# A row-by-row convolution sweep on TensorE: mixed column tiles, a two-row loop and two state slots

## The chip, the core and the metric

One core of a Trainium2 chip runs the kernel. The metric is the device time of one execution in microseconds (us); lower is better. Three executions of the kernel before are given by their median.

## The reference

The model has two layers, on an input of 8 images x 32 channels x 64 x 64 pixels. Layer 0 is a spectral convolution and a mixture of experts over tokens; layer 1 is a convolution in four directional sweeps and the same kind of experts. The change touches the four sweeps alone:

```python
def _sweep(x, w, b, axis, reverse):
    rows = jnp.moveaxis(x, axis, 0)
    if reverse:
        rows = rows[::-1]
    def step(prev, row):
        new = row + jax.nn.relu(_conv1d(prev, w, b))   # 32 channels to 32, 9 taps along the row
        return (new, new)
    _, rest = jax.lax.scan(step, rows[0], rows[1:])
    ...
out = _sweep(x, w_d, b_d, axis=2, reverse=False)
out = _sweep(out, w_u, b_u, axis=2, reverse=True)
out = _sweep(out, w_r, b_r, axis=3, reverse=False)
out = _sweep(out, w_l, b_l, axis=3, reverse=True)
```

A row depends on the row before it, so the 63 steps of a sweep, and the four sweeps, run one after the other.

## The kernel before, in words

Before the sweeps the kernel does layer 0 and the layer norm of layer 1; after them the second mixture of experts. Both parts stay as they are. Each engine has its own program, and semaphores tie them together.

**A row's state.** A row has 64 pixels of 32 channels for 8 images. Four neighbouring pixels (`Q` = 4) lie on the partitions with their channels (4 x 32 = 128), the 16 groups of four (`HO`) lie along the free dimension, with a column of zeros at either side. The state of a row is one of four slots of the tile `state` in SBUF (names print it as RE, of which it is a part), each of 8 images x 18 columns; `state_slot(s, u)` picks the slot by the row's number modulo four.

**A step on TensorE (PE).** The 8 images are two chains of four (`CHAINS`). For a chain, the nine taps become three matmuls of a 128 x 128 banded weight (`conv_sb[:, s, d]`, d = 0, 1, 2) with the previous state shifted by d columns, 4 images x 16 columns = 64 streamed columns. They add up in a PSUM bank (`conv_bank`, two banks a chain, in turns). Each matmul is issued as two column tiles of `OC` = 64 output rows (L717). The data are fp32. The step of a chain waits for the chain's state of the row before (`s_st`) and for the bias in its bank (`s_seed`, L713), and its last matmul raises `s_cv`. PE's program of the sweeps is written out: 4 x 63 rows x 2 chains.

**The other engines.** VectorE (DVE) does one `scalar_tensor_tensor` a chain and row (L1114): relu of the bank plus the row of the source image, into the next state slot; it raises `s_st`. ScalarE (ACT) then writes the bias into the bank that this frees (L851, `seed`). GpSimd (POOL) copies each finished row from its slot to the destination image (L391, `archive`, `s_arc`); in the last sweep ScalarE does it (L865, `s_arl`). Before VectorE writes over a slot, it waits for the archive of the row that was in it, four rows back.

**Between sweeps.** Sweeps 1 and 2 run along the height, 3 and 4 along the width. DMAs issued on SP's queue (L317, `move_rows`, and POOL for some of the last batch) turn the image meanwhile in four batches of 5, 5, 4 and 2 groups of four rows (`MOVED`), 16 DMAs each; each batch waits for the rows of sweep 2 that it needs. Sweep 3 starts with a wait for them (`wait_columns`). Behind sweep 4 the result is turned back the same way (L328).

Other lines in the rows below: L454 keeps PE active with bf16 matmuls of 128 columns (`keep_warm`); L508 is the mixing of the spectrum, in column tiles of 64; L636 pools tokens, in column tiles of 64 with 32 streamed columns; L652 spreads one row over 32 output rows; L663 and L669 are the experts' small products, in tiles of 64 and 32 output rows; L492, L532, L583 and L646 are full-width transforms and transposes.

Of the kernel before, what the change touches and what calls it, by code (L numbers as in the profile page):

```python
# [8 lines left out]
B, C, H, W = 8, 32, 64, 64  # L9
P = 128  # L10
# [4 lines left out]
Q = 4  # L15
HO = H // Q
# [4 lines left out]
WRUN = W // NW  # L21
MO = P // 2
CHAINS = ((0, 4), (4, 8))
OC = P // 2
SEEDS = ((0, 1), (1, 2))
KYC = 4
NCH = KY // KYC
# [1 line left out]
WCOLS = 2 * X8 * KYC * 2 * C  # L29
# [11 lines left out]
def build_kernel(nc, x_in, dft, wspec, conv_w, conv_b, gate_w, gate_b, w1, w2, b2, own, out):  # L41
# [5 lines left out]
    with ExitStack() as ctx:  # L47
        def sb(name, shape, dt=F32):
            return ctx.enter_context(nc.sbuf_tensor(name, shape, dt))

        def sem(name):
            return ctx.enter_context(nc.semaphore(name))
# [4 lines left out]
        RE = sb("RE", [P, 3 * WCOLS])  # L57
# [6 lines left out]
        conv_sb = sb("conv_sb", [P, 4, 3, P])  # L64
# [51 lines left out]
        s_st, s_cv = sem("state_ready"), sem("conv_ready")  # L116
        s_seed, s_arc, s_pad = sem("bias_in_bank"), sem("row_archived"), sem("state_zeroed")
        s_bits, s_arl = sem("banks_written"), sem("last_rows_archived")
# [8 lines left out]
        def blk(region, n):  # L127

            return region[:, n * P:(n + 1) * P]

        def banks(b0, nb):
            return PS[:, b0:b0 + nb, :].rearrange("p k c -> p (k c)")
# [21 lines left out]
        X3 = RA[:, :].rearrange("p (k t i w o) -> p k t i w o", k=NW, t=BH, i=Q, w=WRUN)  # L154


        state = RE[:, 2 * WCOLS + 3072:2 * WCOLS + 3072 + 4 * B * (HO + 2)].rearrange(
            "p (s b v) -> p s b v", s=4, b=B)

        def by_run(ap, k):  # L160

# [96 lines left out]
        def row_count(s, t):  # L258

            return 127 * (s // 2) + 63 * (s % 2) + t + 1  # L260

        def state_count(s, t, c):

            return len(CHAINS) * (row_count(s, t) - 1) + c + 1

        def seed_of(c):

            return next(i for i, (c0, c1) in enumerate(SEEDS) if c0 <= c < c1)

        def state_slot(s, u):  # L270

            return (u + 3 * (s % 2)) % 4

        def conv_bank(s, u, c):

            b0, b1 = CHAINS[c]
            c0, c1 = SEEDS[seed_of(c)]
            bank = 2 * c0 + (s + u + 1) % 2 * (c1 - c0) + c - c0
            return PS[:, bank, 0:(b1 - b0) * HO].rearrange("p (b v) -> p b v", v=HO)

        def archive_row(eng, s, q, u):

            eng.wait_ge(s_st, state_count(s, Q * q + u, len(CHAINS) - 1))
            return row_at(DST[s], s, q, u), state[:, state_slot(s, u), :, 1:1 + HO]

        def row_at(image, s, q, u):

            if s % 2:
                q, u = HO - 1 - q, Q - 1 - u
            if image is XF:  # L290
                return XF[:, Q * q + u]
            if image is XW:
                return XW[:, u, :, q, :]
            return XV[:, u, :, :, q]
# [8 lines left out]
        def wait_columns(eng, j):  # L303

            share = sum(on_pool(j, i) for i in range(Q))
            eng.wait_ge(s_ph[j], 16 * (Q * len(MOVED) - share))
            eng.wait_ge(s_php[j], 16 * share)
# [101 lines left out]
        def _(pe):  # L409
# [60 lines left out]
            for l in range(2):  # L470
                m = pe.matmul(PS[:, 6 + l, 0:BL * NE], centre, gate_sb[:, l, :], start=True, stop=True)
# [50 lines left out]
            for c in range(NCH):  # L522
# [5 lines left out]
                for w, full, read in ((1, s_t1, s_tmp), (0, s_t0, s_comb)):  # L528
                    if c >= 2:
                        pe.wait_ge(read, c - 1)  # L530
                    for x in range(X8):
                        m = pe.transpose(blk(banks(4 * (c % 2) + 2 * w, 2), x), Z[:, c, x, w], ident)  # L532
# [172 lines left out]
            for bank in range(2 * len(CHAINS)):  # L705
                m = pe.matmul(PS[:, bank, 0:P], warm[:, :], warm[:, :], start=True, stop=True)
            m.then_inc(s_bits, 1)
            for s in range(4):
                def step(q, u):
                    for c, (b0, b1) in enumerate(CHAINS):  # L710
                        pe.wait_ge(s_st, state_count(s, Q * q + u - 1, c))
                        if c == SEEDS[seed_of(c)][0]:
                            pe.wait_ge(s_seed, len(SEEDS) * (63 * s + Q * q + u - 1) + seed_of(c) + 1)  # L713
                        for d in range(3):
                            prev = state[:, state_slot(s, u - 1), b0:b1, d:d + HO]
                            for o in range(0, P, OC):
                                m = pe.matmul(conv_bank(s, u, c)[o:o + OC], conv_sb[:, s, d, o:o + OC], prev,  # L717
                                              start=False, stop=(d == 2), skip_group_check=True)
                        m.then_inc(s_cv, 1)

                for r in range(1, H):
                    step(r // Q, r % Q)

            experts(1)

# [148 lines left out]
        def _(dve):  # L874
# [103 lines left out]
            for g in range(8):  # L978
                dve.wait_ge(s_df, g + 1)
                for o, i in if2_pairs(g):  # L980
                    m = dve.tensor_copy(o, i)
# [112 lines left out]
            for s in range(4):  # L1094
                if s % 2 == 0:
                    if s == 0:
                        dve.wait_ge(s_pad, 1)
                        dve.wait_ge(s_fd, 16)
                    else:
                        wait_columns(dve, 0)  # L1100
                    for b0, b1 in CHAINS:
                        dve.tensor_copy(state[:, 0, b0:b1, 1:1 + HO], row_at(SRC[s], s, 0, 0)[:, b0:b1, :]).then_inc(s_st, 1)  # L1102
                else:
                    dve.wait_ge(s_arc, 63 * (s - 1) + 62)

                def step(q, u):
                    for c, (b0, b1) in enumerate(CHAINS):
                        r = Q * q + u
                        dve.wait_ge(s_cv, len(CHAINS) * (63 * s + r - 1) + c + 1)
                        if c == 0 and s == 3 and r > Q:  # L1110
                            dve.wait_ge(s_arl, r - Q)
                        elif c == 0 and 63 * s + r > Q:
                            dve.wait_ge(s_arc, 63 * s + r - Q)
                        dve.scalar_tensor_tensor(out=state[:, state_slot(s, u), b0:b1, 1:1 + HO], in0=conv_bank(s, u, c),  # L1114
                                                 scalar=0.0, in1=row_at(SRC[s], s, q, u)[:, b0:b1, :],
                                                 op0=ALU.max, op1=ALU.add).then_inc(s_st, 1)

                for r in range(1, H):
                    if s == 2 and r < Q:
                        wait_columns(dve, r)  # L1120
                    step(r // Q, r % Q)
# [71 lines left out]
```

## Time and profile before

| | us |
|---|---|
| Median of three executions | 623.08 (619.97 to 624.44) |
| Profiled execution, whole | 622.25 |
| Profiled execution, span from first to last instruction | 620.4 |
| PE busy | 565.0 |
| VectorE busy | 365.3 |
| ScalarE busy | 318.9 |
| GpSimd busy | 95.2 |
| Mean granted clock of TensorE, share of 2.4 GHz | 0.961 |

Times in the profile are us from the span's start, unless marked ns. "PE" is a matmul's record, "PEld" that of a weight load. A record of a matmul lasts from its start to its modelled end, so records of matmuls that follow one another overlap, and the sum of a group is counted without the overlap. Where instructions of one line are merged in an order of time, the row gives the first start and the time to the last end, and xN counts the records.

### The profile page before, as it was taken

The numbers are of one execution on the slowest core, as the hardware profiler recorded it, in microseconds if no ns is written. First come the engines' busy times: TensorE is split into PE (matmuls) and PEld (weight loads), VectorE is DVE, ScalarE is ACT, GpSimd is POOL, SyncE is SP. The second block draws the span as 40 slices with busy tenths as digits, with TensorE's granted clock in tenths as the row PEclk, the third lists the DMA queues.
The fourth block names the chain that finished last, engine by engine and source line by source line (L and its number), as shares of the span: only waits on it lengthen the run. The fifth ranks groups of instructions, "written<-read, shape, count | busy, mean of one in ns | idle before, by whom it ended". The sixth has DMA issues, their size and how long they took to land.

```text
span 620.4 us, 22679 instructions
## 1 busy us (share of the span) xinstructions
PE 565.0 (91%) x9860; PEld 505.4 (81%) x9860; DVE 365.3 (59%) x825; ACT 318.9 (51%) x842; POOL 95.2 (15%) x218
## 2 busy tenths in 40 slices
PE   8978887999997999996999999939999999985997
PEld 8978787999996986896888888838888888974873
DVE  3647989656549825555455445515555545598626
ACT  4766988542368401254444444414445777659510
POOL 4000000000021000000333333333332033320000
PEclk9999999999998889998999999969999999987979
DMA  9830772060000000000000013340000144500007
GB/s 357 318 136 1 274 287 125 1 271 1 1 2 2 1 21 1 0 1 0 5 4 4 4 39 75 83 85 4 5 3 5 33 78 75 97 1 1 2 3 270
DMA packets 52650, 41.53 MB, mean 67 GB/s; under 512 B 47558, under 2 KB 47686, under 8 KB 51334
## 3 DMA queue, kind: packets, MB, share of 16 engines
q1 hardware_dynamic: 52024, 39.10, 19.6%
q8 instruction: 79, 1.29, 0.9%
q0 software_dynamic: 384, 0.59, 0.5%
q10 hardware_dynamic: 144, 0.39, 0.2%
q14 instruction: 19, 0.16, 0.1%
HBM read 27.49 MB, written 4.19 MB: 51 GB/s over the span
## 4 chain that ended last, share of the span: by engine, by line
PE 73%; DVE 16%; ACT 5%; SPq 3%; issue 2%; POOL 1%; DMA 0%; ACTq 0%
PE PS L717 35%; PE PS L433 6%; PE PS L686 5%; DVE RB L958 4%; PE PS L454 4%; SPq L317 3%; PE PS L508 3%; DVE sums L997 3%; PE PS L636 3%; PE PS L583 2%; PE PS L532 2%; DVE RCD L1009 2%; PE PS L539 2%; PE PS L553 2%; PE PS L613 2%
## 5 line engine op out<-in xcount | busy, mean ns | idle before, releaser
L717 PE MATMUL PS<-RE,conv_sb 128*64 128x64 f32 x6048 | 229.3, 226 | 11.2 <-DVE RE L1102 9.2
L717 PEld LDWEIGHTS PS<-RE,conv_sb 128*64 128x64 f32 x6048 | 198.8, 138 | 41.7 <-DVE RE L1102 9.8
L851 ACT COPY PS<-convb_sb 128x64 f32<-128x64 f32 x504 | 108.1, 215 | 117.9 <-DVE RE L1114 77.9
L1114 DVE SCALAR_TENSOR_TENSOR RE<-PS,RCD 128x64 f32<-128x64 f32 x252 | 56.7, 225 | 57.0 <-PE PS L717 40.5
L391 POOL COPY RCD<-RE 128x128 f32<-128x128 f32 x126 | 37.3, 296 | 176.8 <-DVE RE L1114 176.8
L1114 DVE SCALAR_TENSOR_TENSOR RE<-PS,RE 128x64 f32<-128x64 f32 x126 | 32.3, 258 | 29.2 <-PE PS L717 19.4
L780 ACT COPY RB<-PS 32x256 f32<-32x256 f32 x64 | 41.9, 655 | 6.9 <-PE PS L492 6.1
L1114 DVE SCALAR_TENSOR_TENSOR RE<-PS,RB 128x64 f32<-128x64 f32 x126 | 28.4, 225 | 28.1 <-PE PS L717 19.9
L958 DVE COPY RB<-PS 32x256 f32<-32x256 f32 x64 | 41.7, 652 | 5.1 <-PE PS L492 4.3
L454 PE MATMUL PS<-warm 128*128 128x128 bf16 x468 | 38.1, 254 | 7.1 <-ACT RCD L820 4.4
L454 PEld LDWEIGHTS PS<-warm 128*128 128x128 bf16 x468 | 35.0, 116 | 8.1 <-ACT RCD L820 4.7
L508 PE MATMUL PS<-RE,RB 128*64 128x64 f32 x1024 | 32.2, 223 | 8.7 <-DVE RCD L967 3.7
L884 DVE TENSOR_REDUCE sums<-RE 128x32 f32<-128x1024 f32 x16 | 19.4, 1218 | 33.8 <-ACT RE L752 33.8
L508 PEld LDWEIGHTS PS<-RE,RB 128*64 128x64 f32 x1024 | 31.0, 138 | 10.0 <-issue 5.4
L752 ACT ACTIVATE RE<-PS 128x1024 f32<-128x1024 f32 x16 | 16.2, 1021 | 33.6 <-PE PS L433 33.5
L384 POOL TENSOR_TENSOR RE<-RA 128x1024 f32<-128x1024 f32 x3 | 5.7, 1892 | 177.4 <-ACT RA L813 177.4
L433 PEld LDWEIGHTS PS<-dft_sb,RCD 128*128 128x128 f32 x128 | 30.5, 328 | 0.9 <-issue 0.5
L433 PE MATMUL PS<-dft_sb,RCD 128*128 128x128 f32 x128 | 30.8, 396 | 0.0
L741 ACT COPY RCD<-PS 128x256 f32<-128x256 f32 (+1 forms) x40 | 24.7, 692 | 11.1 <-PE PS L697 6.0
L686 PE MATMUL PS<-RCD,espread 128*128 128x512 f32 x64 | 30.4, 631 | 0.0
L799 ACT COPY RB<-PS 128x512 f32<-128x512 f32 (+1 forms) x24 | 16.2, 736 | 26.1 <-PE PS L539 26.1
L613 PE MATMUL PS<-proj,RA 128*128 128x192 f32 x128 | 23.5, 346 | 3.0 <-DVE RA L334 2.6
(118 smaller groups left out, 773.9 us busy)
## 6 DMA issues: line engine op xcount, KB each, us to landing
RE<-wspec SPq DMA_DIRECT2D x8, 2048.0 KB, 8.3
RA<-x_in SPq DMA_DIRECT2D x8, 512.0 KB, 7.6
RCD<-x_in SPq DMA_DIRECT2D x1, 4096.0 KB, 13.4
out<-RA SPq DMA_DIRECT2D x8, 512.0 KB, 2.7
RCD<-RB SPq DMA_DIRECT2D x58, 64.0 KB, 2.6
RE<-RCD SPq DMA_DIRECT2D x32, 80.0 KB, 2.6
RE<-RCD SPq DMA_DIRECT2D x16, 64.0 KB, 2.1
conv_sb<-conv_w SPq DMA_DIRECT2D x1, 768.0 KB, 20.0
```

The lines of the kernel that those rows point to most:

```text
L391: pool.tensor_copy(o, i).then_inc(s_arc, 1)
L433: m = pe.matmul(blk(ln_slot(g), n), src, centre, start=True, stop=True)
L454: pe.matmul(PS[:, bank, 0:P], warm[:, :], warm[:, :], start=True, stop=True)
L508: m = pe.matmul(o[:, x % 2, y], XB[:, c % 2, x, 2 * y + a].rearrange("p r q b -> p (r q b)"), WR[:, c % 3, a, x, y, :], start=True, stop=True)
L613: m = pe.matmul(PS[:, 4 * (g % 2) + n // 2, 192 * (n % 2):192 * (n % 2) + 192], src, proj[:, l, :], start=True, stop=True)
L686: pe.matmul(PS[:, 4 + k % 4, :], espread[:, BL * bh:BL * bh + BL, :].rearrange("p b o -> p (b o)"), rhs, start=True, stop=True).then_inc(s ...
L717: m = pe.matmul(conv_bank(s, u, c)[o:o + OC], conv_sb[:, s, d, o:o + OC], prev, start=False, stop=(d == 2), skip_group_check=True)
L741: m = act.copy(o, i)
L780: m = act.copy(o, i)
L851: act.copy(banks_of, convb_sb[:, s:s + 1].unsqueeze(2).to_broadcast([P, c1 - c0, n])).then_inc(s_seed, 1)
L958: m = dve.tensor_copy(o, i)
L1114: dve.scalar_tensor_tensor(out=state[:, state_slot(s, u), b0:b1, 1:1 + HO], in0=conv_bank(s, u, c), scalar=0.0, in1=row_at(SRC[s], s, q, u ...
```

## The change

`OC`, the output rows of a column tile, becomes a tuple: the matmul of d = 0 is issued as four tiles of 32, those of d = 1 and 2 stay two tiles of 64. PE's program of a sweep becomes row 1, written out, and a hardware loop of 31 passes over two rows each, in which the numbers waited for are worked out from the loop's register. As the slot's address must be fixed within the loop's body, the state has two slots instead of four, and VectorE waits for the archive of two rows back. The whole diff:

```diff
--- before.py
+++ after.py
@@ -21,7 +21,7 @@
 WRUN = W // NW
 MO = P // 2
 CHAINS = ((0, 4), (4, 8))
-OC = P // 2
+OC = (P // 4, P // 2, P // 2)
 SEEDS = ((0, 1), (1, 2))
 KYC = 4
 NCH = KY // KYC
@@ -154,8 +154,8 @@
         X3 = RA[:, :].rearrange("p (k t i w o) -> p k t i w o", k=NW, t=BH, i=Q, w=WRUN)
 
 
-        state = RE[:, 2 * WCOLS + 3072:2 * WCOLS + 3072 + 4 * B * (HO + 2)].rearrange(
-            "p (s b v) -> p s b v", s=4, b=B)
+        state = RE[:, 2 * WCOLS + 3072:2 * WCOLS + 3072 + 2 * B * (HO + 2)].rearrange(
+            "p (s b v) -> p s b v", s=2, b=B)
 
         def by_run(ap, k):
 
@@ -269,7 +269,7 @@
 
         def state_slot(s, u):
 
-            return (u + 3 * (s % 2)) % 4
+            return (u + s) % 2
 
         def conv_bank(s, u, c):
 
@@ -706,20 +706,22 @@
                 m = pe.matmul(PS[:, bank, 0:P], warm[:, :], warm[:, :], start=True, stop=True)
             m.then_inc(s_bits, 1)
             for s in range(4):
-                def step(q, u):
+                def step(r, odd=1):
                     for c, (b0, b1) in enumerate(CHAINS):
-                        pe.wait_ge(s_st, state_count(s, Q * q + u - 1, c))
+                        pe.wait_ge(s_st, state_count(s, r - 1, c))
                         if c == SEEDS[seed_of(c)][0]:
-                            pe.wait_ge(s_seed, len(SEEDS) * (63 * s + Q * q + u - 1) + seed_of(c) + 1)
+                            pe.wait_ge(s_seed, len(SEEDS) * (63 * s + r - 1) + seed_of(c) + 1)
                         for d in range(3):
-                            prev = state[:, state_slot(s, u - 1), b0:b1, d:d + HO]
-                            for o in range(0, P, OC):
-                                m = pe.matmul(conv_bank(s, u, c)[o:o + OC], conv_sb[:, s, d, o:o + OC], prev,
+                            prev = state[:, (s + odd - 1) % 2, b0:b1, d:d + HO]
+                            for o in range(0, P, OC[d]):
+                                m = pe.matmul(conv_bank(s, odd, c)[o:o + OC[d]], conv_sb[:, s, d, o:o + OC[d]], prev,
                                               start=False, stop=(d == 2), skip_group_check=True)
                         m.then_inc(s_cv, 1)
 
-                for r in range(1, H):
-                    step(r // Q, r % Q)
+                step(1)
+                with pe.Fori(1, H // 2) as pair:
+                    step(2 * pair, 0)
+                    step(2 * pair + 1, 1)
 
             experts(1)
 
@@ -1107,10 +1109,10 @@
                     for c, (b0, b1) in enumerate(CHAINS):
                         r = Q * q + u
                         dve.wait_ge(s_cv, len(CHAINS) * (63 * s + r - 1) + c + 1)
-                        if c == 0 and s == 3 and r > Q:
-                            dve.wait_ge(s_arl, r - Q)
-                        elif c == 0 and 63 * s + r > Q:
-                            dve.wait_ge(s_arc, 63 * s + r - Q)
+                        if c == 0 and s == 3 and r > 2:
+                            dve.wait_ge(s_arl, r - 2)
+                        elif c == 0 and 63 * s + r > 2:
+                            dve.wait_ge(s_arc, 63 * s + r - 2)
                         dve.scalar_tensor_tensor(out=state[:, state_slot(s, u), b0:b1, 1:1 + HO], in0=conv_bank(s, u, c),
                                                  scalar=0.0, in1=row_at(SRC[s], s, q, u)[:, b0:b1, :],
                                                  op0=ALU.max, op1=ALU.add).then_inc(s_st, 1)
```

## Rows read from the trace of the kernel before

**Rows 1.** The page: busy time by engine, and the chain that ended last by line.

```profile
PE 565.0 (91%) x9860; PEld 505.4 (81%) x9860; DVE 365.3 (59%) x825; ACT 318.9 (51%) x842; POOL 95.2 (15%) x218
...
PE PS L717 35%; PE PS L433 6%; PE PS L686 5%; DVE RB L958 4%; PE PS L454 4%; SPq L317 3%; PE PS L508 3%; DVE sums L997 3%; PE PS L636 3%; PE PS L583 2%; PE PS L532 2%; DVE RCD L1009 2%; PE PS L539 2%; PE PS L553 2%; PE PS L613 2%
```

**Rows 2.** Stretches (length, busy PE, PEld, DVE, ACT, POOL, PEclk, DMA, GB/s).

```profile
291.70:403.90 112.20, 112.08 (x3002) 97.73 (x3004) 56.05 (x250) 53.85 (x252) 36.69 (x124) 1.00 0.12 30
403.90:413.80 9.90, 0.83 (x24) 0.69 (x24) 0.83 (x5) 0.75 (x4) 4.37 (x9) 0.77 0.45 102
413.80:531.90 118.10, 116.36 (x3024) 100.35 (x3024) 60.80 (x253) 67.47 (x310) 30.44 (x68) 0.98 0.19 32
```

**Rows 3.** The page's costliest groups: busy, mean ns | idle before, releaser.

```profile
L717 PE MATMUL PS<-RE,conv_sb 128*64 128x64 f32 x6048 | 229.3, 226 | 11.2 <-DVE RE L1102 9.2
...
L851 ACT COPY PS<-convb_sb 128x64 f32<-128x64 f32 x504 | 108.1, 215 | 117.9 <-DVE RE L1114 77.9
L1114 DVE SCALAR_TENSOR_TENSOR RE<-PS,RCD 128x64 f32<-128x64 f32 x252 | 56.7, 225 | 57.0 <-PE PS L717 40.5
...
L1114 DVE SCALAR_TENSOR_TENSOR RE<-PS,RE 128x64 f32<-128x64 f32 x126 | 32.3, 258 | 29.2 <-PE PS L717 19.4
```

**Rows 4.** Instructions in order of time, four narrow windows from 310.48 to 311.22.

```profile
310.31 0.23 DVE L1114 SCALAR_TENSOR_TENSOR RE<-PS,RCD 128x64 f32<-128x64 f32 x1 [0.32 <-PE PS L717]
...
310.39 0.47 PE L717 MATMUL PS<-RE,conv_sb 128*64 128x64 f32 x3
...
310.59 0.14 PEld L717 LDWEIGHTS PS<-RE,conv_sb 128*64 128x64 f32 x2
...
310.66 0.23 DVE L1114 SCALAR_TENSOR_TENSOR RE<-PS,RCD 128x64 f32<-128x64 f32 x1
310.70 0.46 PE L717 MATMUL PS<-RE,conv_sb 128*64 128x64 f32 x10
...
310.95 0.30 POOL L391 COPY RCD<-RE 128x128 f32<-128x128 f32 x1 [0.60 <-DVE RE L1114]
...
311.21 0.23 DVE L1114 SCALAR_TENSOR_TENSOR RE<-PS,RCD 128x64 f32<-128x64 f32 x1 [0.32 <-PE PS L717]
```

**Rows 5.** In order of time, PE: one group of L508, one of L583.

```profile
87.39 3.95 PE L508 MATMUL PS<-RE,RB 128*64 128x64 f32 x128
...
152.62 1.95 PE L583 MATMUL PS<-dft_sb,RB 128*128 128x128 f32 x16
```

**Rows 6.** In order of time: changes of tile width; clock at the last.

```profile
110.05 0.43 PE L508 MATMUL PS<-RE,RB 128*64 128x64 f32 x8
...
110.41 0.14 PEld L532 LDWEIGHTS PS<-dft_sb,RCD 128*128 128x128 f32 x1
...
598.87 0.36 PE L669 MATMUL PS<-hid,w_sb 128*32 128x8 f32 x4
...
599.16 0.10 PEld L454 LDWEIGHTS PS<-warm 128*128 128x128 bf16 x1
...
588.87 0.40 PE L652 MATMUL PS<-rs_row,ones 1*32 1x128 f32 x2
...
589.20 0.20 PEld L636 LDWEIGHTS PS<-RE,RB 128*64 128x64 f32 x4 [0.20 <-issue]
...
588.60:589.30 0.70, 0.70 (x10) 0.34 (x7) 0.32 (x1) 0.00 (x0) 0.00 (x0) 1.00 0.00 0
```

**Rows 7.** Line L713: durations in ns (min/median/max), first and last start.

```profile
L713 PEldq EVENT_SEMAPHORE  x504: 51/51/51, 291.7 to 531.0; - x168
```

**Rows 8.** SP's issues from 398.15 on; waits (us, times, longest) at 403:421.

```profile
398.22 19.76 SPq L317 DMA_DIRECT2D RE<-RCD  x26
...
DVE RE L1102 <- DMA RE<-RCD: 8.6, 1, 8.6
...
DVE RE L1114 <- DMA RE<-RCD: 4.0, 3, 1.9
```

**Rows 9.** Busy time and granted clock, 597.1 to 599.1 us (columns as rows 2).

```profile
597.10:599.10 2.00, 2.00 (x36) 1.80 (x33) 0.00 (x0) 0.00 (x0) 0.00 (x0) 0.50 0.04 8
```

## The prediction

> **What bounds the kernel now.** I read the page first, then the sweeps' windows, then single instructions of one row. TensorE is busy for 91% of the span, and the sweep's matmuls, L717, alone are 35% of the chain that ended last [rows 1]. The four sweeps last from 291.7 to 403.9 us and from 413.8 to 531.9 us, and the stretch in between is a wait for DMAs [rows 2, 8]. In the sweeps PE shows as busy all the time [rows 2], with 6048 matmul records of 221 ns [rows 3], and the reader must not stop there: the records overlap, so a full PE row says nothing of how fast instructions start.
>
> Single instructions say it. In a row at 310.4 us, chain 1's last matmul starts at 310.39 and takes 221 ns; VectorE's instruction on it starts at 310.66 and ends at 310.89; the row's archive copy starts at 310.95. Chain 0's VectorE instruction ends at 310.54 (310.31 + 0.23) and its next weight load starts at 310.59, while PE had started no matmul since 310.39 [rows 4]. So PE has a hole of some 0.20 us in each row, and each chain of images runs in its own closed loop: release to first weight load 0.05; weights to first matmul 0.05 (load at 310.59, the second pass at 310.70, less 0.058); six passes 0.058 apart with two tiles side by side, 5 x 0.058 + 0.007 = 0.30; drain of the last matmul 0.22; hand-over to VectorE 0.05; VectorE 0.225. Sum 0.895 us, and VectorE's starts agree (310.31, then 311.21). The 0.058 is from L508, which has the same tile shape: 64 pairs of tiles start within 3.95 - 0.22 = 3.73 us [rows 5]. PE itself is taken for 2 x 0.35 = 0.70 us of the 0.895. The third sweep's VectorE instruction takes 258 instead of 225 ns [rows 3], so a row there is 0.929 us.
>
> **Column tiles, first matmul of a step.** Instructions: an fp32 matmul leaves two load/matmul pairs (6048 records for 252 x 2 x 3 x 2 calls). A chain's step goes from 12 to 16 pairs. Gain: the exposed weight load halves. L652 loads 32 columns; it starts at 588.87 and its second and last pass starts at 589.27 - 0.27 = 589.00, 0.13 later [rows 6]. A pass of 128 columns is some 0.11 apart from the next (L583: (1.95 - 0.27) / 15 [rows 5]), and the clock was full [rows 6], so that load took 0.02 to 0.03 against 0.05 for 64 columns: 0.02 us a row. Later loads hide behind passes in either shape. The fourth tile starts 3 x 0.007 after the first where the second started 0.007 after it, which takes 0.014 back. Net gain between 0.01 and 0.023 us a row.
>
> Cost: the array changes its tile width inside each step (32 to 64 columns) and again between the chains' steps (64 to 32). At each change of width in this trace, PE stands still [rows 6]. 64 to 128: the last L508 matmul starts at 110.05 + 0.43 - 0.22 = 110.26, the next load at 110.41, 0.15 later. 32 to 128: L669 (a 0.20 record) at 598.87 + 0.36 - 0.20 = 599.03, L454's load at 599.16, 0.13, and L454 there waits for no semaphore. 32 to 64: L652 at 589.00, load at 589.20, 0.20, of which its 128 streamed columns are 0.05 more than 64; the trace names "issue" as what it waited for. Within one width the next load starts within 0.01 of the matmul. L652 also has one row, so no row shows 32 against 64 columns at 128 rows, which is what the change makes. Bounds for one switch: nothing, and 0.20 us. I take 0.15, by the nearest rows with 32 or 64 streamed columns.
>
> The Trainium skill, page "TensorEngine Tiling (Array Packing)", section "Key Properties", says that changing the tiling mode, and not merely the tile, drains TensorE. The rows above agree as far as they go. By that rule both switches are paid and the time is the forecast below; without it, it is rival (a).
>
> A chain's step on PE then is: load 0.03; four tiles, two passes, 0.058 + 3 x 0.007 = 0.08; switch 0.15; load 0.05; four passes 3 x 0.058 + 0.007 = 0.18; together 0.49 us to its last matmul, and 0.15 to the next chain's load: 0.64. (If eight pairs in four tiles go no faster than two tiles' mean of 0.029 a pair, the 0.08 becomes 0.20 and a row 0.25 longer; I take 0.08, since tiles start 0.007 apart [rows 4].) Two chains: 1.27 us a row. The closed loop would be 0.49 + 0.22 + 0.05 + 0.225 + 0.05 = 1.04. So the limit moves from the loop to PE, and a row takes 1.27.
>
> Sum: three sweeps of 63 rows at 1.272 - 0.896 = 0.376, 71.1 us; the third at 1.272 - 0.929 = 0.343, 21.6 us; together 92.7.
>
> Taken back around it. Sweep 2's last two batches of row moves are issued on SP without a gap from 398.2 to 418 us, 0.65 us each [rows 8]. The third batch is released 8 rows before the end of the sweep; with rows 0.376 longer the sweep ends 3.0 us later against that queue, and the 8.6 us wait for columns shrinks by as much. The 4.0 us of DMA waits in the next three rows swallow another 1.0. The last column moves behind sweep 4, issued on the same queue, give perhaps 1 us in the same way (an estimate from the 3.0). Net 92.7 - 5 = 88.
>
> **Two state slots.** VectorE now waits for the archive of row r - 2. Row r - 2 was archived 0.36 us after its state was done (310.89, 310.95 + 0.30 = 311.25), and the chain 0 instruction after the next (311.21 + 0.895) starts near 312.1, so the wait is met 0.85 us early [rows 4]; ScalarE's copies in sweep 4 stand behind its seeds of 0.215 [rows 3]; with a copy as long as GpSimd's 0.30 it is still some 0.7 us early. Longer rows add to it. Cost nothing; a missing cover would queue the chain 1 instruction, its seeds and its archive behind it.
>
> **The loop of two rows.** No row has a wait against a register or a taken branch. PE has 504 semaphore instructions in the sweeps at 51 ns [rows 7], today not in the closed loop, since a load starts 0.05 after VectorE's end. Now each chain's two waits need sums on the sequencer. Bounds: zero, if the sequencer runs ahead; three such 51 ns instructions per step in the loop, 0.15 us. In the forecast PE is the limit, and the next chain's state is ready at 0.22 + 0.05 + 0.225 + 0.05 = 0.545 after its own last matmul, 0.09 before PE's 0.64 are over. So 0.09 of the 0.15 is covered and 0.06 a step, 0.12 a row (30 us), is the worst; I take zero and keep the rest for the range. Queued behind such a wait is all of that chain's step and, PE being in order, the other chain's.
>
> Forecast: 622.25 + 88 = 710 us on the profiled execution's own time, which lies 0.8 below the median of 623.08.
>
> **Rivals.** (a) No drain between 32 and 64 columns, and register waits hidden: both are widths of a divided array, and the only 32 to 64 row in the trace also changes its rows. Then 0.01 to 0.023 us a row are gained, 252 rows give 2.5 to 5.8 us: about 618, not slower. It decides if one switch costs under about 0.02 us. (b) No drain, but the waits enter the closed loop: 252 x (0.15 - 0.01) = 35, less 2 at the SP queue: 655. (c) Only the switch inside the step drains: loop 1.04 beats PE's 2 x 0.49, so 189 x 0.14 + 63 x 0.14 (VectorE's 258 ns count again) = 36, less 2: 656. (d) With PE standing still more, its clock falls to the lower level, 1.2 GHz: the granted clock was 0.50 from 597.1 to 599.1 us, after L663's and L669's short matmuls [rows 9]. For it speaks that, in the sum above, PE streams for less of a row; against it, the clock is 1.00 in the sweeps even now with holes [rows 2]. Passes and loads would double, 0.34 a step: some 0.68 x 252 = 170 more, 880.
>
> The Trainium skill, page "TensorE: Matmul & The Clock Gate", section "Wait — 56ns, not 53.3ns?", says that matmuls never start less than about 25 ns apart. The sweep's rows have tiles 7 ns apart, so the trace does not bear it out for separate tiles; by the rule the four tiles' two passes would take 0.18 and the row 0.19 more.
>
> **How the numbers follow.** Forecast's mechanism 60%, with a range of its own of 690 to 750 (each of a row's four switches 0.02 shorter: 20 us less; waits exposed: 30 more, and 0.01 on each switch). Rivals (b) and (c) together 18%; (a) 20%; (d) 2%. To leave out no more than two in ten the range runs from 640 to 755. A measurement of this kernel tells about 1% from no change. Faster by over 1% would need 6.2 us, above (a)'s upper bound, 0.04; within 1%, 0.16; slower, 0.80.
>
> **What would show it.** Right: at the sweep's matmuls a load of 64 columns that starts 0.15 us after the last 32-column matmul, and one of 32 columns 0.15 after the last of 64; VectorE's starts 1.27 apart per chain; 8064 records; less of the wait at 404 us. Wrong: rows at 0.88 with no hole between widths (a), holes ahead of the first load only, longer than 0.05 after VectorE's end (b), a hole only inside the step (c), PEclk near 5 in the sweeps (d).

## The result and the profile after

The changed kernel takes 891.54 us (median of four executions, 889.3 to 894.49) against 622.79 us (619.97 to 624.44, four) for the kernel before: a ratio of 1.4322, with a 95% interval of 1.4282 to 1.4362. The forecast was 710, its range ended at 755. What happened is rival (d), to which the prediction gave 2% and 880 us. The profiled execution took 892.41 us.

The page of the changed kernel: its busy time, the granted clock in 40 slices, the chain by line, and the groups of the sweep's matmul, its weight load and VectorE's instruction.

```profile
PE 842.4 (95%) x11876; PEld 668.1 (75%) x11876; DVE 364.8 (41%) x825; ACT 319.4 (36%) x842; POOL 94.1 (11%) x218
...
PEclk9999999998999555555555555555555555558798
...
L717 PE MATMUL PS<-RE,conv_sb 128*32 128x64 f32 (+1 forms) x8064 | 503.5, 321 | 4.8 <-DVE RE L1104 4.1
L717 PEld LDWEIGHTS PS<-RE,conv_sb 128*32 128x32 f32 (+1 forms) x8064 | 358.7, 179 | 149.6 <-issue 85.9
...
L1116 DVE SCALAR_TENSOR_TENSOR RE<-PS,RCD 128x64 f32<-128x64 f32 x252 | 56.5, 224 | 195.7 <-PE PS L717 195.7
```

Busy PE rose from 565.0 [rows 1] to 842.4 us, and VectorE's instruction, 224 ns against 225 [rows 3], now has 195.7 instead of 57.0 us of idle time ahead of it. The clock row tells the rest at a glance: 5 in every slice from the start of the sweeps to their end. The mean length of a matmul's record goes with it, from 226 [rows 3] to 321 ns. The stretches of the changed kernel (columns as in rows 2) show the same number by number.

```profile
288.00:291.00 3.00, 1.37 (x30) 0.98 (x32) 0.52 (x3) 1.82 (x8) 0.00 (x0) 1.00 0.00 0
291.00:292.50 1.50, 1.50 (x32) 1.10 (x32) 0.26 (x2) 0.43 (x2) 0.29 (x1) 0.55 0.00 0
...
291.70:541.00 249.30, 249.30 (x3994) 177.71 (x3991) 55.78 (x249) 53.75 (x250) 36.62 (x125) 0.50 0.06 15
541.00:549.00 8.00, 3.64 (x64) 2.52 (x62) 1.24 (x5) 0.64 (x3) 4.60 (x9) 0.50 0.35 61
549.00:801.00 252.00, 251.67 (x3993) 180.03 (x3990) 62.83 (x252) 67.45 (x309) 31.65 (x70) 0.50 0.08 14
```

The sweeps begin near 290 us. The clock is 1.00 up to 291 us, 0.55 in the next 1.5 us, and 0.50, TensorE's lower level of 1.2 GHz, for the 509 us from 291.7 to 801. All four executions have a mean clock of 0.69 to 0.694, so it fell in each. The stretch of 249.3 us holds 249 VectorE instructions, two a row: 2.00 us a row, where it was 0.896.

Single instructions of one chain's step, from three narrow windows of the changed kernel's timeline:

```profile
350.10 0.57 PE L717 MATMUL PS<-RE,conv_sb 128*64 128x64 f32 x3
350.35 0.13 PEld L717 LDWEIGHTS PS<-RE,conv_sb 128*32 128x32 f32 x1
...
350.35 0.44 PE L717 MATMUL PS<-RE,conv_sb 128*32 128x64 f32 x8
...
350.72 0.19 PEld L717 LDWEIGHTS PS<-RE,conv_sb 128*64 128x64 f32 x2 [0.17 <-issue]
...
351.10 0.57 PE L717 MATMUL PS<-RE,conv_sb 128*64 128x64 f32 x3
351.35 0.13 PEld L717 LDWEIGHTS PS<-RE,conv_sb 128*32 128x32 f32 x1
```

The chain's first load is at 350.35, the next chain's at 351.35: 1.00 us a step. The eight 32-column matmuls end at 350.79; with a record of 0.31 us the last of them starts at 350.48, and the first 64-column load comes at 350.72, 0.24 later. The step's last 64-column matmuls start at 351.10, the load behind them 0.25 later. The holes stand where the prediction put them, but are longer than its 0.15, since the clock is down.

The taken-back term, from the waits of 535 to 560 us (total, times, longest; columns as in rows 8):

```profile
DVE RE L1104 <- DMA RE<-RCD: 3.6, 1, 3.6
DVE RE L1116 <- DMA RE<-RCD: 1.6, 1, 1.6
```

The wait for columns fell from 8.6 to 3.6 us, the DMA waits behind it from 4.0 to 1.6 [rows 8].

The sum closes. Four sweeps of 63 rows at 2.00 us are 504 us; before they were 189 x 0.896 + 63 x 0.929 = 228. The difference of 276, less the 5.0 + 2.4 taken back, is 269; the profiled executions differ by 892.41 - 622.25 = 270.

### The profile page after: what moved, and what is told of

Same layout as the page of the kernel before. It is cut to its first block, busy times and chain, and to the rows that moved or that the text cites. A ratio compares the mean times of both kernels' runs of the same rounds, so it can differ in the third digit from the quotient of the medians.

```text
span 890.6 us, 27461 instructions
## 1 busy us (share of the span) xinstructions
PE 842.4 (95%) x11876; PEld 668.1 (75%) x11876; DVE 364.8 (41%) x825; ACT 319.4 (36%) x842; POOL 94.1 (11%) x218
## 4 chain that ended last, share of the span: by engine, by line
PE 82%; DVE 11%; ACT 3%; issue 1%; DMA 1%; POOL 0%; SPq 0%; ACTq 0%
PE PS L717 56%; PE PS L433 4%; PE PS L686 3%; DVE RB L960 3%; PE PS L508 2%; DVE sums L999 2%; PE PS L636 2%; PE PS L454 2%; PE PS L583 2%; PE PS L532 2%; DVE RCD L1011 2%; PE PS L613 2%; PE PS L539 1%; PE PS L553 1%; PE PS L414 1%
## 5 line engine op out<-in xcount | busy, mean ns | idle before, releaser
L717 PE MATMUL PS<-RE,conv_sb 128*32 128x64 f32 (+1 forms) x8064 | 503.5, 321 | 4.8 <-DVE RE L1104 4.1
L717 PEld LDWEIGHTS PS<-RE,conv_sb 128*32 128x32 f32 (+1 forms) x8064 | 358.7, 179 | 149.6 <-issue 85.9
L1116 DVE SCALAR_TENSOR_TENSOR RE<-PS,RCD 128x64 f32<-128x64 f32 x252 | 56.5, 224 | 195.7 <-PE PS L717 195.7
L508 PE MATMUL PS<-RE,RB 128*64 128x64 f32 x1024 | 33.6, 228 | 8.5 <-DVE RCD L969 3.6
L508 PEld LDWEIGHTS PS<-RE,RB 128*64 128x64 f32 x1024 | 32.5, 143 | 9.8 <-DVE RB L960 5.1
L391 POOL COPY RB<-RE 128x128 f32<-128x128 f32 x63 | 18.5, 293 | 107.7 <-DVE RE L1116 107.7
L613 PE MATMUL PS<-proj,RA 128*128 128x192 f32 x128 | 25.9, 369 | 3.0 <-DVE RA L334 2.6
L613 PEld LDWEIGHTS PS<-proj,RA 128*128 128x128 f32 x128 | 24.8, 220 | 4.0 <-DVE RA L334 2.9
```

The lines of the kernel that those rows point to most:

```text
L391: pool.tensor_copy(o, i).then_inc(s_arc, 1)
L508: m = pe.matmul(o[:, x % 2, y], XB[:, c % 2, x, 2 * y + a].rearrange("p r q b -> p (r q b)"), WR[:, c % 3, a, x, y, :], start=True, stop=True)
L613: m = pe.matmul(PS[:, 4 * (g % 2) + n // 2, 192 * (n % 2):192 * (n % 2) + 192], src, proj[:, l, :], start=True, stop=True)
L717: m = pe.matmul(conv_bank(s, odd, c)[o:o + OC[d]], conv_sb[:, s, d, o:o + OC[d]], prev, start=False, stop=(d == 2), skip_group_check=True)
```

## The experiments

Open were: which of the three parts costs what; whether the forecast's sum would be right at full clock; why the clock falls and, above all, why it stays down. Times are medians of four to ten executions, but of two for e2, e4, e5, e6, e7 and e13, and a single one for e10 and e11; where a ratio stands, it is to the kernel before, timed beside it, with its 95% interval.

**The parts alone.** First the loop and the two slots without the mixed widths, and the mixed widths in the written-out program of before with its four slots.

```diff
# e1, against the changed kernel
-OC = (P // 4, P // 2, P // 2)
+OC = (P // 2, P // 2, P // 2)
# e2, against the kernel before
-OC = P // 2
+OC = (P // 4, P // 2, P // 2)
-                            for o in range(0, P, OC):
+                            for o in range(0, P, OC[d]):
```

> All three matmuls of a step as two tiles of 64, with the loop and the two slots kept. Theory (changes of tile width drain PE, and the clock falls with them): rows of 0.90 us, PEclk 1.00 in the sweeps, 620 to 625 us. Rival (the waits against registers and the branch enter the closed loop): 0.05 to 0.15 us more a row, 635 to 660 us.

> The mixed tiles alone, with PE's program written out and four slots. Theory (the tiles are the whole loss): 885 to 895 us, rows of 2.00 us, PEclk 0.50 in the sweeps. Rival (the loop or the slots carry a part of it): well below, 710 us or less if they are what lets the clock fall.

Measured: e1 637.52 us, ratio 1.0231 (1.0169 to 1.0292). e2 893.33 us, 1.4335 (1.4222 to 1.4448). So the mixed widths alone make the whole loss, and the loop with its slots costs some 15 us (10 to 18 by the interval) that don't show beside them. e2 is written out, so neither the loop nor its register waits bring the clock down. From a stretch of e2:

```profile
350.00:400.00 50.00, 50.00 (x804) 35.55 (x806) 11.26 (x50) 10.79 (x51) 7.41 (x26) 0.50 0.01 2
```

50 VectorE instructions in 50 us: 2.00 us a row again.

**The slots alone, and where the loop's 15 us are.**

```diff
# e9, against the kernel before: the diff's state slots and nothing else
-            return (u + 3 * (s % 2)) % 4
+            return (u + s) % 2
...
-                        if c == 0 and s == 3 and r > Q:
-                            dve.wait_ge(s_arl, r - Q)
+                        if c == 0 and s == 3 and r > 2:
+                            dve.wait_ge(s_arl, r - 2)
# e12, against e1: ten rows in the loop's body, six passes and two rows behind
-                with pe.Fori(1, H // 2) as pair:
-                    step(2 * pair, 0)
-                    step(2 * pair + 1, 1)
+                with pe.Fori(1, 7) as ten:
+                    for k in range(10):
+                        step(10 * ten - 8 + k, k % 2)
+                step(62, 0)
+                step(63, 1)
```

> The kernel before with two state slots instead of four, nothing else. Theory (the archive of two rows back is done 0.85 us before it is needed): no difference, 620 to 625 us, rows of 0.896 us. Rival (the wait binds somewhere, in the last sweep above all, where ScalarE archives): rows of sweep 4 longer by 0.05 us or more, 626 us or more.

> All tiles 64, two slots, but PE's loop has ten rows in its body and runs six times a sweep (with the rows left over written out): 24 passes in all instead of 124. Theory (the 15 us that the loop of two rows costs are spent at each return of the loop, 0.12 us each): 3 us above the kernel before, 623 to 628 us. Rival (the waits against registers cost it, in every row): 637 us, as with two rows.

Measured: e9 622.01 us, 0.9977 (0.9949 to 1.0004); e12 624.14 us, 1.0006 (0.9977 to 1.0035). Two slots cost nothing. VectorE's instructions in e1, in order of time:

```profile
330.44 0.58 DVE L1116 SCALAR_TENSOR_TENSOR RE<-PS,RCD 128x64 f32<-128x64 f32 x2 [0.32 <-PE PS L717]
331.47 0.58 DVE L1116 SCALAR_TENSOR_TENSOR RE<-PS,RCD 128x64 f32<-128x64 f32 x2 [0.45 <-PE PS L717]
332.36 0.58 DVE L1116 SCALAR_TENSOR_TENSOR RE<-PS,RCD 128x64 f32<-128x64 f32 x2 [0.32 <-PE PS L717]
333.39 0.57 DVE L1116 SCALAR_TENSOR_TENSOR RE<-PS,RCD 128x64 f32<-128x64 f32 x2 [0.45 <-PE PS L717]
```

and in e12:

```profile
331.39 0.57 DVE L1118 SCALAR_TENSOR_TENSOR RE<-PS,RCD 128x64 f32<-128x64 f32 x2 [0.32 <-PE PS L717]
332.28 0.57 DVE L1118 SCALAR_TENSOR_TENSOR RE<-PS,RCD 128x64 f32<-128x64 f32 x2 [0.32 <-PE PS L717]
333.28 0.57 DVE L1118 SCALAR_TENSOR_TENSOR RE<-PS,RCD 128x64 f32<-128x64 f32 x2 [0.43 <-PE PS L717]
```

In e1 rows of 0.89 and 1.03 us take turns: each return of the loop, every second row, adds 0.14. The row that is worked out from a register without a return, the second of the body, takes 0.89 as ever. e12 has the same register waits in nearly every row but 24 returns instead of 124; one of them shows in the row from 332.28 to 333.28, and the kernel loses nothing that can be measured. So the price is the return, 15 us / 124 = 0.12 us each, and the register waits are free. The trace has the return's instructions, in e1 (ns, min/median/max):

```profile
L722 PEldq COMPARE_BRANCH  x124: 76/208/240, 295.6 to 547.1; - x124
```

**Is it the clock, and does the forecast's sum hold at full clock?** Two matmuls on unused data behind each chain's step, into a bank that nothing reads, give PE more to stream; e7 has half the columns. They are added work, in PE's own time. e5 turns chain 1's order to d = 1, 2, 0, so that a row has two changes of width where it had four.

```diff
# e4, against the changed kernel (e7: 0:MO in place of 0:P and of the last :)
                         m.then_inc(s_cv, 1)
+                        for o in range(0, P, MO):
+                            pe.matmul(PS[o:o + MO, 6, 0:P], conv_sb[:, s, 2, o:o + MO], conv_sb[:, s, 0, :],
+                                      start=True, stop=True)
# e5, against the changed kernel
-                        for d in range(3):
+                        for d in ((0, 1, 2), (1, 2, 0))[c]:
```

> As the changed kernel, plus one matmul behind each step of a chain (two tiles of 64 rows, 128 streamed columns, fp32, into an unused bank; its result is not used): more work, to give the array more to stream. Theory (half of the loss is the lower clock, which follows how little the array streams between drains): the clock returns to 1.00, a chain's step takes 0.64 + 0.21 = 0.85, rows 1.70 us, 820 us. Rival (the clock falls because of the changes of width themselves, whatever is streamed): clock 0.50, rows 2.0 + 0.86 = 2.86 us, 1110 us.

> As the run with extra streams, but 64 columns instead of 128 in the extra matmul. Theory (streaming share): if it is enough for the clock, rows of 2 x (0.64 + 0.12) = 1.52 us and 770 to 775 us; if not, PEclk 0.50 and rows of 2 x (1.00 + 0.21) = 2.43 us, 1000 us.

> Chain 1 takes its matmuls in the order d = 1, 2, 0, so that it ends in tiles of 32, as chain 0 begins, and begins in tiles of 64, as chain 0 ends: the same instructions, two changes of width a row instead of four. Theory (each change of width is a drain, 0.15 us at full clock): two drains and the share of PE's time that they take go away; PE's part of a row is 1.27 - 0.20 to 0.30, so the closed loop of about 1.0 us sets the row, and if the clock stays 1.00 the run takes 645 to 670 us. Rival (the clock falls all the same, rows near 1.6 us with PEclk 0.50): 770 to 800 us. Rival (changes are free and the narrow tiles or a mixed order are slow): 890 us, unchanged.

Measured: e4 818.33 us, 1.3131 (1.3032 to 1.3231), clock 1.00 in the sweep, 1.70 us a row. e7 767.62 us, 1.2336 (1.2278 to 1.2395), 1.00, 1.495 us a row. e5 670.13 us, 1.077 (1.0721 to 1.0818), 1.00, rows of 1.03, and 1.17 at the loop's returns. More work made the kernel 73 and 124 us faster than the changed one: the time lost beyond the forecast is the clock's. e5's row of 1.03 is what the prediction worked out for a chain with the switch inside its step alone (1.04, rival (c)'s row); there the loop's return shows again, since PE no longer sets the row.

**Why does it stay down: what streams now, or what it was before?** e13 adds e4's matmuls in sweeps 1 and 3 alone; sweeps 2 and 4 are the changed kernel's own rows. e15 adds them in rows 1 to 11 of sweeps 1 and 3 alone.

```diff
# e13, against e4
-                        for o in range(0, P, MO):
+                        for o in range(0, P if s % 2 == 0 else 0, MO):
# e15, against e4
+                ahead = 11 if s % 2 == 0 else 1
+                for r in range(1, ahead + 1):
+                    step(r, r % 2, s % 2 == 0)
+                with pe.Fori((ahead + 1) // 2, H // 2) as pair:
```

> The changed kernel with the extra matmuls of 128 columns in sweeps 1 and 3 only; sweeps 2 and 4 are the changed kernel's own, entered at full clock. Theory A (the mixed tiles can't hold the clock, wherever they start from): rows of 2.00 us and PEclk 0.50 in sweeps 2 and 4, 855 us. Theory B (they can hold it but not win it back once it has fallen at the start of the sweeps): rows of 1.27 us and PEclk 1.00 in sweeps 2 and 4, 765 us.

> The changed kernel with the extra matmuls of 128 columns behind the steps of rows 1 to 11 of sweeps 1 and 3 alone (22 of 252 rows); the loop's body is the changed kernel's own. Theory B (a row of mixed tiles holds the full clock once it has it, and can't win it back): PEclk 1.00 in all four sweeps, rows of 1.262 us after the first eleven, 705 to 720 us. If the clock is lost again within the sweeps: rows of 2.00 us from there on, more than 750 us.

Measured: e13 764.48 us, 1.2259 (1.2197 to 1.2321); e15 717.97 us, 1.1511 (1.1467 to 1.1555). e13's four sweeps (columns as in rows 2):

```profile
292.00:398.00 106.00, 106.00 (x2448) 72.92 (x2444) 27.46 (x123) 26.24 (x122) 18.05 (x61) 0.98 0.00 0
400.00:478.00 78.00, 78.00 (x1985) 58.26 (x1980) 27.64 (x123) 26.42 (x124) 18.05 (x62) 1.00 0.17 42
488.00:595.00 107.00, 107.00 (x2522) 73.87 (x2517) 32.34 (x127) 27.32 (x127) 18.38 (x62) 1.00 0.01 1
600.00:678.00 78.00, 77.67 (x1872) 59.22 (x1868) 30.55 (x119) 39.81 (x174) 15.27 (x10) 1.00 0.28 47
```

In sweeps 2 and 4 the changed kernel's own rows run at a clock of 1.00 for the whole of 78 us each. e15 shows how the clock came back (its stretches):

```profile
292.50:294.00 1.50, 1.50 (x32) 0.91 (x32) 0.32 (x2) 0.43 (x2) 0.29 (x1) 0.67 0.00 0
294.00:296.00 2.00, 2.00 (x31) 1.50 (x32) 0.22 (x1) 0.21 (x1) 0.00 (x0) 0.50 0.04 8
296.00:300.00 4.00, 4.00 (x94) 2.59 (x90) 1.12 (x5) 0.88 (x5) 0.59 (x2) 0.95 0.00 0
...
311.00:380.00 69.00, 69.00 (x1755) 51.49 (x1755) 24.29 (x109) 23.45 (x109) 15.91 (x54) 1.00 0.00 1
470.00:625.00 155.00, 155.00 (x3914) 115.01 (x3910) 57.73 (x241) 65.31 (x300) 29.14 (x64) 1.00 0.12 21
```

The clock falls to 0.50 in the sweep's first rows in e15 as in the changed kernel and e2, and climbs within 4 us under the added matmuls. From row 12 on nothing is added, and it stays at 1.00. The same rows thus run at either level, by the one at which they begin: they hold a full clock, and in no run did they win back one that had fallen.

The fall itself is not the mixed widths' doing. e9, with tiles of 64 alone and 622 us, has it too in its profiled execution, in the same place:

```profile
291.00:292.50 1.50, 1.35 (x32) 1.27 (x34) 0.45 (x2) 0.79 (x6) 0.10 (x1) 0.85 0.00 0
292.50:294.00 1.50, 1.50 (x34) 1.50 (x32) 0.45 (x2) 0.41 (x3) 0.27 (x2) 0.50 0.00 0
294.00:296.00 2.00, 2.00 (x47) 1.92 (x44) 0.73 (x4) 0.73 (x4) 0.51 (x2) 0.64 0.04 8
296.00:300.00 4.00, 4.00 (x114) 3.69 (x114) 1.96 (x9) 1.96 (x10) 1.36 (x5) 1.00 0.01 4
```

Its rows of one width bring the clock back by 296 us, and nothing of it shows in the time. The fall is not in every execution: in those of the kernel before and of e1 the clock stays at 1.00 through the sweep's first rows.

Between sweeps 2 and 3 it falls in the kernel before as well, as the stretches of before already show: 0.77 for the wait for columns and 0.98 for the stretch of sweeps 3 and 4 [rows 2]. Looked at closely, the kernel before stands at 0.50 from 410 to 418 us, while PE has nothing to do and in sweep 3's first rows, and is back at 1.00 from 420 on. In e13 and e15 too the clock is at 0.50 in sweep 3's first rows (485 to 487 and 462 to 466 us), although matmuls are added there. So a changed kernel that had kept its clock in sweeps 1 and 2 would most likely have lost it here for the rest; no run shows that by itself.

Nor does every mixture of widths stay down. e5 has the changed kernel's instructions with two changes a row and no added work. Its clock falls in the same place, and comes back:

```profile
294.00:296.00 2.00, 2.00 (x44) 1.71 (x44) 0.45 (x2) 0.54 (x3) 0.51 (x2) 0.50 0.03 8
296.00:300.00 4.00, 3.92 (x110) 3.11 (x110) 1.54 (x7) 1.29 (x6) 0.88 (x3) 0.88 0.00 0
300.00:305.00 5.00, 5.00 (x152) 4.04 (x153) 2.06 (x10) 1.96 (x10) 1.18 (x4) 1.00 0.00 0
```

What doesn't bring the clock back is the changed kernel's row, with four changes, and of 2.00 us at the lower clock; e5's row takes 1.64 us there.

VectorE's starts in e15:

```profile
340.28 0.23 DVE L1121 SCALAR_TENSOR_TENSOR RE<-PS,RCD 128x64 f32<-128x64 f32 x1 [0.40 <-PE PS L717]
340.91 0.22 DVE L1121 SCALAR_TENSOR_TENSOR RE<-PS,RCD 128x64 f32<-128x64 f32 x1 [0.41 <-PE PS L717]
341.54 0.23 DVE L1121 SCALAR_TENSOR_TENSOR RE<-PS,RCD 128x64 f32<-128x64 f32 x1 [0.41 <-PE PS L717]
342.17 0.23 DVE L1121 SCALAR_TENSOR_TENSOR RE<-PS,RCD 128x64 f32<-128x64 f32 x1 [0.41 <-PE PS L717]
```

0.63 a chain, 1.26 a row, with no step at the loop's return. The 22 rows with added work take 1.70 instead of 1.26, 9.7 us, and the first few of each eleven longer still, while the clock is down. Without the added work e15 would stand at about 708, an estimate, where the forecast was 710.

The switches at full clock, from e13's sweep 2 (four narrow windows):

```profile
430.26 0.32 PE L717 MATMUL PS<-RE,conv_sb 128*32 128x64 f32 x8
...
430.51 0.13 PEld L717 LDWEIGHTS PS<-RE,conv_sb 128*64 128x64 f32 x1
...
430.67 0.29 PE L717 MATMUL PS<-RE,conv_sb 128*64 128x64 f32 x4
...
430.89 0.11 PEld L717 LDWEIGHTS PS<-RE,conv_sb 128*32 128x32 f32 x1
```

The eight end at 430.58, so the last started at 430.36 (records of 0.22), and the load of 64 columns comes 0.15 later. The group of 64-column matmuls ends at 430.96, so its last started at 430.74, and the next chain's load comes 0.15 later.

**One width, but a slower chain.** If PE's idle share as such kept the clock down, a kernel with one width and a longer wait on VectorE should show it. Unused VectorE instructions ahead of each of the sweep's own make the closed loop longer in the kernel before. Each of the added ones waits for the one before it.

```diff
# e6: one instruction of 256 elements, as here; e10: two, of 256 and 160; e11: two of 256
+                        dve.wait_ge(s_junk, len(CHAINS) * (63 * s + r - 1) + c)
+                        dve.tensor_tensor(rstd[:, :], sums[:, :], sums[:, :], ALU.add).then_inc(s_junk, 1)
                         dve.wait_ge(s_cv, len(CHAINS) * (63 * s + r - 1) + c + 1)
```

> The kernel before (one width, no loop) with an extra vector instruction of 256 elements (unused result) ahead of each one of the sweep, so that VectorE sets the row at some 1.2 to 1.3 us: the same streaming per row as the changed kernel would have at full clock, and no change of width. Theory (the clock follows how much PE streams of the time): PEclk falls to 0.50 in the sweeps. Rival (the clock falls only because of changes of width): PEclk 1.00. Time near 710 us either way, as VectorE sets the row.

> The kernel before, one tile width, with two extra vector instructions (256 and 160 elements, unused results) ahead of each one of the sweep: VectorE sets the row at about 1.25 us, what the mixed tiles would take at full clock. Theory (the clock falls because PE streams too small a part of the row, as in the changed kernel): PEclk 0.50 in the sweeps, rows of 1.25 to 1.30 us, about 710 us. Rival (it is the changes of width that bring the clock down): PEclk 1.00, rows of 1.25 us, about 708 us.

> The same with 256 and 256 elements, rows of about 1.41 us. Theory: PEclk 0.50 here even if the run before it holds the clock. Rival: PEclk 1.00. About 748 us either way.

Measured: e6 647.59 us, 1.0407 (1.0359 to 1.0456), but its rows came to 0.93 us only, so it told nothing. e10 819.13 us (one execution), rows of 1.65 us instead of 1.25. e11 869.13 us (one execution), rows of 1.85. All three missed the length meant. e10 from 300 to 350 us:

```profile
300.00:350.00 50.00, 34.26 (x727) 25.84 (x721) 47.96 (x183) 12.93 (x61) 12.72 (x31) 1.00 0.01 3
```

and e11's clock by slices:

```profile
PEclk9999999998999666685566655655555765688898
```

So rows of one width can fail to hold the clock too, when PE waits long (e11, one execution); there it goes up and down, where in the changed kernel's rows it never came up. Nor do these runs rule out that all hangs on how much PE does in a microsecond. Records can't be compared as they stand: e10's 727 in 50 us are twelve a step, e2's 804 are sixteen, and a step is six passes in both. In passes e10, at full clock, did 363 and e2, at 0.50, did 301.

The rows without added work can be put side by side by their length at the lower clock, each with the same twelve passes. Rows of 1.28 us (e9, one width), 1.64 (e5, two changes) and 1.65 (e10, one width): after each fall the clock was back at 1.00 within some 10 us of PE's start. Rows of 1.85 (e11, one width): it was at 0.50 most of the time, once from 552 to 680 us, and at 1.00 for some 6 us at a time. Rows of 2.00 (the changed kernel and e2, four changes): it never came back. e10, with one width, and e5, with two, have rows of nearly the same length there and behave alike. No run has one width and rows of 2.00 us, so whether the four changes keep the clock down by the time they take, or in another way too, is not shown.

**32 columns for all three, which takes the changes of width out.**

```diff
# e8, against the kernel before (written out, four slots)
-OC = P // 2
+OC = P // 4
# e3, against the changed kernel (loop of two rows, two slots); e14 the same, against e12 (ten rows)
-OC = (P // 4, P // 2, P // 2)
+OC = (P // 4, P // 4, P // 4)
```

> All three matmuls as four tiles of 32, loop and slots kept: narrow tiles, no change of width. Theory (the changes of width cost, not the narrow tiles): no drain inside a row, clock full, rows of 0.87 to 0.91 us, 615 to 626 us. Rival (four narrow tiles are slow by themselves, 0.029 us a pair at best): 24 pairs a chain take 0.70 us, a row 1.4 us, some 750 us.

> The kernel before with all tiles of 32 rows: no loop, four slots, one width. Theory (only the first load is exposed, it is halved, and the fourth tile starts later): rows of 0.890 against 0.896 us, 1.5 us faster than the kernel before, 619 to 622 us. Rival (the sequencer can't feed 96 load/matmul pairs a row): 640 us.

> All tiles 32 (96 load/matmul pairs a row and a half more than either kernel) with a loop of ten rows, six passes a sweep. Theory (written out, the kernel with tiles of 32 lost its 138 us to the fetching of instructions; in a loop that fits there is none to fetch, and 24 returns cost 3 us): rows of 0.890 us, 621 to 626 us. Rival (the sequencer can't issue that many pairs): over 650 us.

Measured: e3 642.46 us, 1.031 (1.0247 to 1.0373); e8 760.05 us, 1.2208 (1.2156 to 1.226); e14 645.65 us, 1.0358 (1.0307 to 1.041). There is no hole between tiles, and none of them stays at the lower clock: the hole belongs to the change of width, and tiles of 32 as such don't keep the clock down. But all three missed their forecasts. e3's rows take 0.89 and some 1.06 us in turn, so its excess is the loop's return, 0.17 each here. The page of e8:

```profile
q8 instruction: 126, 2.06, 1.1%
...
L717 PE MATMUL PS<-RE,conv_sb 128*32 128x64 f32 x12096 | 245.6, 226 | 127.5 <-issue 117.5
```

and PE in order of time in e8:

```profile
333.24 2.44 PE L717 MATMUL PS<-RE,conv_sb 128*32 128x64 f32 x126 [1.55 <-issue]
336.99 2.43 PE L717 MATMUL PS<-RE,conv_sb 128*32 128x64 f32 x125 [1.31 <-issue]
340.95 1.27 PE L717 MATMUL PS<-RE,conv_sb 128*32 128x64 f32 x54 [1.52 <-issue]
```

Every 126 matmuls or so, and as many loads, PE stands for 1.3 to 1.6 us and waits for nothing but issue; 117.5 us in all. The kernel's instruction queue moved 126 packets; e14's moved 50, and that of the kernel before, written out without such holes, 79. PE's start of sweep 1 in e14, in order of time:

```profile
302.62 2.46 PE L717 MATMUL PS<-RE,conv_sb 128*32 128x64 f32 x123 [1.98 <-issue]
306.80 1.67 PE L717 MATMUL PS<-RE,conv_sb 128*32 128x64 f32 x83 [1.71 <-issue]
```

The same holes, in the first pass of the loop alone, 14.4 us of idle time by issue in the whole kernel; in later passes rows take 0.89. That the engine waits there for its code is the reading that fits e3, e8 and e14 (holes with new code, none with code run before), but it is argued: no run changed the code's size by itself. With twice the matmuls a row, the written-out program didn't keep up here, and a loop did. Of the gain of the shorter first load, forecast at 0.01 to 0.023 us a row, these kernels' regular rows show 0.007 (0.889 for 0.896).

No variant beat the kernel before; e9 and e12 equal it.

## Why the prediction was wrong, by its own steps

- **The bound** was read rightly: a closed loop per chain before, and PE behind the change. With mixed widths a chain's step on PE is what a row is made of.
- **Cost of a switch**, 0.15 out of a range from nothing to 0.20: right at full clock, 0.15 for either direction, by e13. The two rows that came nearest before, 64 to 128 and 32 to 128 [rows 6], had 0.15 and 0.13.
- **Length of a step**: 0.64 forecast, 0.631 at full clock (row 1.26 against 1.27). Load 0.03, passes, load 0.05 and four passes as worked out.
- **Taken back**: 5 us forecast, of which 3.0 at the wait for columns and 1.0 behind it; 5.0 and 2.4 measured, on rows longer than forecast.
- **Two slots**: nothing, shown by e9.
- **A reading**: the prediction takes 221 ns from rows 3 for a matmul's record; those rows give 226, the mean, and 221 is the median. Nothing in the sum changes by it.
- **The loop**: taken for nothing, with up to 0.12 us a row if uncovered. In a row of mixed widths it is covered (e15, even steps of 0.63). Uncovered it costs 15 us, within the bound. The place was wrong: not the register sums ahead of the waits, which e12 shows to be free, but the return of the loop, for which the prediction had no term.
- **The step that failed** is the weighing of rival (d), at 2%, and with it the 60% for a forecast at full clock. The argument was "against it, the clock is 1.00 in the sweeps even now with holes [rows 2]". It misreads the rows: they give 1.00 for sweeps 1 and 2, but 0.77 for the wait behind them and 0.98 for sweeps 3 and 4. The clock falls in the kernel before as well, and its rows bring it back. The prediction asked whether the new rows would hold a full clock, and they do (e13, e15). It left out whether they would win back one that had fallen, and they don't: 0.50 for 509 us, some 183 us of the time.
- **Rival (d)'s own sum** was near: 880 against 891.5, a row of 1.95 against 2.00. It reckoned 0.34 a step for passes and loads that double; measured are 0.37: six passes' spacing and the loads add 0.18 net, and the two switches, which it left at 0.15, add 2 x 0.095, since they grow to 0.24 with the clock.
- The forecast's own sum, 710, describes the changed kernel at full clock. e15, with eleven rows of added work at the start of two sweeps, runs at 718, of which 9.7 us or a little more are that work. Between some 708 and 891.5 stand 183 us of clock.

Still open: what the changed kernel's rows lack to win the clock back, and why it falls at the start of the first sweep in some executions, with one width (e9) as with two, and not in others (the kernel before, e1).

## What to carry to other kernels

Keep one tile width through a chain of small dependent matmuls, or put steps of like width side by side: a change of width cost 0.15 us here, three weight loads of 64 columns, to save half of one, and going from four changes a row to two took 221 us off (e5). Before a change that puts holes into PE's stream, work out the time at both clock levels and look in the profile for places where the clock already falls, a wait for DMAs above all; a kernel whose rows hold a full clock may not regain it after a fall, and eleven rows of denser streaming at the start of two sweeps were worth 174 us here (891.5 to 718.0). Written-out code can have a price that a profile before does not show: twice the loads and matmuls a row cost 138 us (e8). A loop with ten rows in its body paid it in its first pass only (e14), and nothing measurable for its returns (e12).

## What was unexpected of the hardware

- The granted clock has two lasting levels for the same instructions: 0.50 for some 509 us (after), 1.00 for 155 us (e15's stretch from 470 to 625, the first 13 us of it with added matmuls), by the clock at which the stretch began.
- Added matmuls made a kernel faster: 891.5 us without, 767.6 with two more matmuls of 64 streamed columns a step (e7).
- A switch of width lengthens with the clock, from 0.15 to 0.24 us, less than twofold; passes go from 0.058 to about 0.11 us.
- PE stood 1.3 to 1.6 us about every 252 instructions in e8, 117.5 us in all, while the kernel before, with half as many loads and matmuls a row, shows 11.2 us of idle time in the same group [rows 3].
- A hardware loop's return on PE cost 0.12 to 0.14 us where nothing covered it (e1), and 0.17 with twice the instructions in its body (e3).
